# A kernel's constants lose their own block: the first tile's transfers lead the program, the attention weights load during the first sweep

## What is computed

```python
h = jnp.maximum(_layernorm(x), 0.0);  x = x + L0(h, adj)   # d*(adj+I)*d @ h @ W.T + b
h = jnp.maximum(_layernorm(x), 0.0);  x = x + L1(h, adj)   # relu(d*(adj+I)*d @ (h @ weight))
h = jnp.maximum(_layernorm(x), 0.0);  x = x + L2(h, adj)   # two steps of diffusion and of nucleus
...                                                        # attention, with W1, W2, W3, U1, U2, U3, gamma, beta
h = jnp.maximum(_layernorm(x), 0.0);  x = x + L3(h, adj)   # (1-t)*(h @ weight) + t*(adj @ (h @ weight))
```

## Time and profile before

| | |
|---|---|
| time, median of 3 runs | 3471.04 us (3469.64 to 3474.25) |
| the profiled execution: its time, its span | 3468.18 us, 3466.4 us |
| mean granted TensorE clock | 0.959 of full speed |
| TensorE (PE) busy | 3137.2 us, 91% of the span |
| VectorE busy | 2444.9 us, 71% |
| GpSimd busy | 2140.7 us, 62% |
| constants' block, from the first transfer's issue to the front block's first | 0.74 to 15.64 us |
| front block | 15.64 to 451.09 us |

### The profile page before, as it was taken

One profiled execution on the slowest core, in us unless ns is written; L12 is line 12 of the kernel. 1 busy time (PEld: TensorE's weight loads), 2 busy tenths in 40 slices (PEclk: granted clock), 3 DMA queues, 4 the chain that ended last, 5 costly groups with the idle time before them and its releaser, 6 DMA issues. The chain is left out here.

```text
span 3466.4 us, 42065 instructions
## 1 busy us (share of the span) xinstructions
PE 3137.2 (91%) x13212; PEld 2267.5 (65%) x13212; DVE 2444.9 (71%) x3401; ACT 1598.2 (46%) x2357; POOL 2140.7 (62%) x4214
## 2 busy tenths in 40 slices
PE   4999999997899999999966698988999999996899
PEld 3888778885567777777754255544566566664788
DVE  6840123333998889888884799999988999998000
ACT  2311322225666666666753455655555555552200
POOL 2212422224788888888880677877888788786211
PEclk9999999998899999999988899999999999998899
DMA  7644344433112222222211111211222222223255
GB/s 258 239 146 146 116 156 166 165 129 87 44 54 59 60 64 58 59 60 64 58 33 63 47 57 48 63 44 55 58 82 75 73 85 82 74 83 103 92 202 173
DMA packets 140702, 327.59 MB, mean 95 GB/s; under 512 B 15456, under 2 KB 93664, under 8 KB 129248
## 3 DMA queue, kind: packets, MB, share of 16 engines
q1 hardware_dynamic: 140512, 325.30, 29.5%
HBM read 286.70 MB, written 38.54 MB: 94 GB/s over the span
## 5 line engine op out<-in xcount | busy, mean ns | idle before, releaser
L1030 ACT ACTIVATE junk<-E,negp 128x3327 uint8<-128x3327 f32 x208 | 637.3, 3064 | 142.8 <-issue 112.0
L1401 DVE SCALAR_TENSOR_TENSOR U<-E,trial 128x3327 f32<-128x3327 f32 x182 | 674.7, 3707 | 0.0
L925 PE MATMUL bank<-big,adj 128*128 128x512 f32 x1352 | 611.4, 603 | 11.2 <-ACT t L1056 11.2
L925 PEld LDWEIGHTS bank<-big,adj 128*128 128x128 f32 x1352 | 253.5, 193 | 333.3 <-issue 332.2
L298 PE MATMUL bank<-big,E 128*128 128x256 f32 x1664 | 364.7, 381 | 1.9 <-PEq L58 1.7
L885 PE MATMUL bank<-Hc,PT 128*128 128x256 f32 x1248 | 303.2, 395 | 66.7 <-ACT PT L1069 66.4
L298 PEld LDWEIGHTS bank<-big,E 128*128 128x128 f32 x1664 | 315.0, 191 | 48.3 <-issue 5.4
L885 PE MATMUL bank<-Hc,adj 128*128 128x256 f32 x1456 | 336.3, 383 | 9.4 <-ACT adj L1069 9.4
L1363 DVE TENSOR_REDUCE nmax<-E 128x1 f32<-128x3327 f32 x52 | 187.9, 3614 | 206.2 <-ACT E L1073 206.2
L885 PEld LDWEIGHTS bank<-Hc,PT 128*128 128x128 f32 x1248 | 244.7, 198 | 127.3 <-ACT PT L1069 77.9
L885 PEld LDWEIGHTS bank<-Hc,adj 128*128 128x128 f32 x1456 | 278.3, 192 | 72.1 <-issue 22.5
(11 more groups left out here) (248 smaller groups left out, 5729.7 us busy)
## 6 DMA issues: line engine op xcount, KB each, us to landing
adj<-adjT SPq DMA_DIRECT2D x131, 448.0 KB, 3.4
E<-adjT SPq DMA_DIRECT2D x32, 1664.0 KB, 6.9
adj<-adjT SPq DMA_DIRECT2D x104, 384.0 KB, 3.3
adj<-adjT SPq DMA_DIRECT2D x20, 1664.0 KB, 6.9
E<-adjT SPq DMA_DIRECT2D x26, 1216.0 KB, 5.7
xt<-xin SPq DMA_DIRECT2D x52, 128.0 KB, 5.6
xt<-x_d SPq DMA_DIRECT2D x52, 128.0 KB, 5.3
xo_d<-xo SPq DMA_DIRECT2D x26, 256.0 KB, 3.7
```

The source lines that it names most:

```text
L925: last = mm(agg[:, 0:w], adj[:, SPAN * (k % 2) + j - AGG[k]], rhs[:, j], start=(j == 0), stop=False)
L1030: go(junk[:, 0:N], E[:, t % DEPTH, 0:N], func, bias=negp[:, t % 2, j:j + 1], scale=1.0, accum_out=acc_[:, t % 2, j:j + 1]).then_inc(summed ...
L1401: V_.scalar_tensor_tensor(out=U[:, 0:N], in0=e, scalar=point, in1=e, op0=ALU.is_ge, op1=ALU.mult, accum_out=found))
```

## The change

The constants' block is removed with its barrier. What it did goes into the front block:

- SP's list now begins with the transfers of the first tile (x 0, adjacency block 0, W0), then x 1, blocks 1 and 2; `wkk` (twice), `a1t`, `a2`, `tb` and W1 follow. `bias0`, `gam`, `bet`, `ua`, `ub`, `uc` are issued one in each round from t = 13 to 18 of the first sweep.
- GpSimd fills the constants at the head of its list of the front block, and waits for the six late loads before the second sweep.
- TensorE waits at first for the constants and W0 alone. It waits for W1 and the attention weights between the sweeps, and multiplies W1 by W2 there, into the PSUM tensor `lg`. VectorE makes `omt` and the two copies into `wqq` there.
- `a1t` and `a2` lie in `E[:, DEPTH - 1]` in place of `adj`.

```diff
-        a1t, a2 = adj[0:A, 0:DC, :], adj[0:A, DC, 0:A]
+        a1t, a2 = square(E[0:A, DEPTH - 1])[:, 0:DC], E[0:A, DEPTH - 1, DC * P:DC * P + A]
...
-        with phase_semaphores(nc) as s:
-            loaded, idz, made, w12, cdone = (s(n) for n in (
-                "c_loaded", "c_ident_zero", "c_made", "c_w12", "c_copied"))
-            with nc.Block() as block:
...
+                    chunked = lambda w: w.rearrange("(c p) f -> p c f", p=P)
+                    late = [(bias0[:], b0.partition_broadcast(P)), (gam[:], gamma.partition_broadcast(P)),
+                            (bet[:], beta.partition_broadcast(P)), (ua[:], chunked(UA)), (ub[:], chunked(UB)), (uc[:], chunked(UC))]
                     load_x(0)
                     load_adj(0)
+                    sp.dma_start(wd[:], chunked(W0T)).then_inc(w0_in, 16)
                     load_x(1)
-                    sp.dma_start(wd[:], W0T.rearrange("(c p) f -> p c f", p=P)).then_inc(w_in, 16)
                     load_adj(1)
                     load_adj(2)
-                    sp.dma_start(w1, W1g.rearrange("(c p) f -> p c f", p=P)).then_inc(w_in, 16)
+                    sp.dma_start(wkk[:, :, 0:A], chunked(A3)).then_inc(qk_in, 16)
+                    sp.dma_start(wkk[:, :, A:2 * A], chunked(A3)).then_inc(qk_in, 16)
+                    sp.dma_start(a1t, A1T.rearrange("a (c p) -> a c p", p=P)).then_inc(qk_in, 16)
+                    sp.dma_start(a2, A2).then_inc(qk_in, 16)
+                    sp.dma_start(tb[:], tin.partition_broadcast(P)).then_inc(tb_in, 16)
+                    sp.dma_start(w1, chunked(W1g)).then_inc(w1_in, 16)
                     for t in range(NT):
+                        if 0 <= t - NT // 2 < len(late):
+                            dst, src = late[t - NT // 2]
+                            sp.dma_start(dst, src).then_inc(late_in, 16)
                         sp.wait_ge(normed, t + 1)
                         load_x(t + 2)
...
                     sp.wait_ge(first_in, 32)
+                    sp.wait_ge(late_in, 16 * len(late))
...
-                    pe.wait_ge(w_in, 32)
+                    pe.wait_ge(consts, 7)
+                    pe.wait_ge(w0_in, 16)
                     for t in range(NT + 1):
...
+                    pe.wait_ge(w1_in, 16)
+                    pe.wait_ge(qk_in, 64)
+                    for c in range(DC):
+                        last = mm(lg[:, 0, c * A:(c + 1) * A], a1t[:, c, :], a2, start=True, stop=True)
+                    last.then_inc(w12, 1)
                     for r in range(NT + 2):
...
                     tt = nc.gpsimd.tensor_tensor
+                    nc.gpsimd.memset(ident[:], 0.0).then_inc(zeroed, 1)
+                    for dst, value in ((ones[:], 1.0), (expo[:], -0.5), (zero[:], 0.0), (ln_const[:, 0:1], -1.0 / D),
+                                       (ln_const[:, 1:2], 1.0 / D), (ln_const[:, 2:3], LN_EPS)):
+                        nc.gpsimd.memset(dst, value).then_inc(consts, 1)
+                    pool.wait_ge(zeroed, 1)
+                    nc.gpsimd.affine_select(out=ident[:], in_=ident[:], compare_op=ALU.not_equal, fill=1.0, base=0,
+                                            pattern=[[-1, P]], channel_multiplier=1).then_inc(consts, 1)
+                    pool.wait_ge(consts, 7)
                     ln_pool(pool, ln, 0, 0)
...
+                    pool.wait_ge(late_in, 16 * 6)
                     for u in range(NT):
...
                     dve.wait_ge(rs_copied, NT)
+                    dve.wait_ge(consts, 7)
...
                     dve.wait_ge(fin, 6)
+                    dve.wait_ge(tb_in, 16)
+                    V_.tensor_scalar(omt[:], tb[:], -1.0, 1.0, ALU.mult, ALU.add).then_inc(fin, 1)
+                    dve.wait_ge(w12, 1)
+                    for half in range(2):
+                        V_.tensor_copy(wqq[:, :, half * A:(half + 1) * A],
+                                       lg[:, 0, 0:DC * A].rearrange("p (c a) -> p c a", c=DC)).then_inc(w12_copied, 1)
+                    dve.wait_ge(w12_copied, 2)
+                    dve.wait_ge(fin, 7)
```

More of the change, by code:

```diff
@@ L419, in build @@
             rsum = tr[:, 0]
-            w_in, first_in = s("w_in"), s("first_in")
+            w0_in, w1_in, first_in = s("w0_in"), s("w1_in"), s("first_in")
+            qk_in, tb_in, late_in = s("qk_weights_in"), s("tb_in"), s("late_in")
+            zeroed, consts, w12, w12_copied = s("ident_zeroed"), s("consts_made"), s("w12"), s("w12_copied")
             adj_in = [s(f"adj_in{k}") for k in range(RING)]
```

## The result

| | before | changed |
|---|---|---|
| median of 3 runs | 3471.04 us | 3450.32 us (3449.36 to 3451.72) |
| profiled span | 3466.4 us | 3447.6 us |
| profiled execution's time | 3468.18 us | 3449.36 us |

The ratio is 0.9938, with a 95% interval of 0.9924 to 0.9952: faster by 20.7 us, where 18.8 were forecast. In two later groups of runs the changed kernel stood at 0.9938 (0.9922 to 0.9955) and 0.9949 (0.9936 to 0.9963) of before, 20.4 and 18.7 us by the medians. By span the gain is 18.8 us, as forecast; the other 1.9 us are the distance between the profiled execution and the median, which was 2.9 us before and is 1.0 us now. That is within the spread of the runs.

The account below looks back on a forecast made before the run. The constants' block, with every engine mostly idle, and then TensorE's wait for W1 were taken to hold up the start. -14.90 - 4.35 + 0.45 = -18.8 us gave 3452.2 us, range 3446 to 3459.

Parts of the forecast that it names:

- The block lies on the path, 14.90 us: Front of the kernel: removing constants' block and barrier moves SP's first front transfer from 15.64 to 0.74, winning 14.90 us.
- The wait for W1, 4.35 us: Tile 0, first sweep: TensorE waiting for W0 alone shrinks the wait behind the row sum from 5.03 to 0.68, 4.35 us.
- The thin cover of block 1: Tile 1, first sweep: adjacency block 1 lands at 13.1, VectorE wants it at 14.6; 1.5 us cover, no loss taken.
- SyncE's issues: First burst: twelve SP issues before its first wait instead of seven, some 0.5 us each; about 1 us later, hidden.
- The late loads, nothing; 4.7 us uncovered: First sweep, rounds 13 to 18: six loads, 1920 KB, stay hidden and cost nothing; 4.7 us with the cover gone.
- the rival: Late loads take queue time from blocks VectorE or TensorE waits for; 4.7 us come back, 3456.9 us; chance 0.07.
- The product, 0.45 us: Between the sweeps: four passes for W1 times W2 in TensorE's full stream cost 0.45 us, ends 0 and 1.15.
- a sign of being wrong: Between the sweeps: a gap of over 1.2 us was listed among observations that would show the prediction wrong.
- The sum: Whole kernel: -14.90 - 4.35 + 0.45 = -18.8 us, taking the median from 3471.0 to 3452.2 us.
- The clock as a rival: Attention block: earlier start moves TensorE's clock drops; ending slower needs 25.7 us given back; chance 0.03 on the slow side.

Follow-up runs that it names:

- the execution of 3485.42 us: One execution of the changed kernel with the wait for W1 put back in front of TensorE's first work; that version measured 3459.23 us, ratio 0.9974.

## Why the prediction was right

- **The block lies on the path, 14.90 us.** Right, with 0.56 us less: SyncE started at 0.74, but block 0 landed 7.98 us after it, where 7.42 had been read off the later burst. In the other profiles with no constants' block that issue x 0 first it was 7.39 to 7.82 us. The block's own length varies as well: in the run with the wait split the front block began at 15.17, so the 14.34 us are good to some 0.5.
- **The wait for W1, 4.35 us.** Right as a size: 18.66 - 14.34 = 4.32 us in the changed kernel, 4.31 us by itself. The run with W1 behind W0 adds what the prediction only half said: the price is that of W1's place behind two blocks, and the wait itself is free.
- **The thin cover of block 1.** Right: no wait in the first profile. In a second profile of the changed kernel VectorE did wait for two later blocks, at 86 and 93 us, 0.2 and 0.4 us, and in the run with the product five times 1.36 us at 94: there the cover of blocks is thin too, which the prediction did not look at. VectorE waited 0.30 us for block 1 as soon as tile 0 came 1.8 us sooner. The 4.2 us that block 1 was said to need behind W0 should be 4.1 at 409 KB/us, or 4.4 with x 1, which is issued before it.
- **SyncE's issues.** Wrong without harm: the issue of x 2 took 6.5 us, not 0.5. It was hidden, which the run with the small loads in rounds shows.
- **The late loads, nothing; 4.7 us uncovered.** Nothing was right, and the price of the rival was too low: without cover they held block 1 back 7.0 us and cost VectorE 5.4 to 5.7.
- **The product, 0.45 us.** Mis-sized: 0.89, with a gap of 1.32 us that lies beyond the 1.2 which the prediction gave as a sign of being wrong. The passes cost the 0.45; another 0.44 us came with their being there, which the row of two warm passes could not show, and whose cause stays open.
- **The sum.** By terms the changed kernel earned 14.34 + 4.32 - 0.89 = 17.8 us by its own mechanisms. That the span fell by exactly the forecast 18.8 us is luck: the rest is 0.4 us in the first sweep, partly VectorE's stall in the kernel before, and 0.6 us in later stages whose code is the same.
- **The clock as a rival.** It did not end on the slow side. But its mechanism is real at a smaller size, up to 3 us by layer 1's start, from execution to execution. And the execution of 3485.42 us, at a clock of 0.948, lost 26 us, the size that the prediction said this rival needs; it was one of the ten of its version, and none of the 12 executions of the changed kernel itself did so. The Trainium skill's page "TensorE: Matmul & The Clock Gate", Part 1, says that the period over which activity is judged runs freely; that fits a state which changes between executions of one kernel, as 1.00 and 0.82 in two profiles of the changed kernel did, and no run here proves it.

## What to carry to other kernels

Here a set-up stage before the first transfer of the main loop cost its whole length, however small its work: put the first tile's transfers at the head of the queue, and the rest where the loop has room. Order transfers by the time at which they are first waited for, and remember that one wait for two of them is as late as the later one; a load of 256 KB at the wrong place cost 4 to 6 us, and 1920 KB cost 5.4 to 5.7 us in the burst and nothing that shows in the middle of the loop. A small product belongs where its engine has slack: in TensorE's full stream four passes cost 0.89 us, in tile 8 of the first sweep nothing.

## What the runs showed of the hardware

- A stage's length followed TensorE's granted clock at its start. In all fourteen profiles, layer 1 took 333.1 to 333.5 us with 1.00 in its first 8 us (nine), 334.8 to 335.1 with 0.80 to 0.82 (two), and 335.7 to 336.5 with 0.64 to 0.66 (three), the same instructions each time. With three products a round in the idle gaps before it the clock was 1.00 there too, in the one profile taken.
- SyncE needed 6.5 us to issue the thirteenth transfer of a burst, when of the twelve before it only x 0 had landed. With six before it the same transfer took 0.33 us, and with the same twelve in another order 0.43.
- The late loads, with rows of 1 to 2 KB, held the queue for longer than their bytes say: 1920 KB pushed a block back by 7.0 us, where blocks moved at 409 KB/us. That the rows are the reason was not tried.
- A pass of an fp32 product with its own load of 128 weights took 0.11 us in a full stream with 2 or with 64 columns, and 0.21 us with 256.
